# A fused metaformer block: the experts' bias as one 512-column product whose weights come back from DRAM, two small VectorE steps given to ScalarE, and the top-2 mask made in one step

## The reference

```python
t = _to_tokens(x)                                  # pixels x 128 channels
n = _ln_t(t)                                       # layer norm over channels
router_probs = softmax(n @ router_w + router_b)    # 8 experts
top_p, top_i = top_k(router_probs, 2)
top_p = top_p / sum(top_p)
expert_out = einsum('bnd,edc->bnec', n, expert_w) + expert_b
t = t + einsum('bnk,bnkc->bnc', top_p, take_along_axis(expert_out, top_i))
```

## Time and profile before

| | |
|---|---|
| time, median of 3 runs | 4167.12 us (4166.49 to 4171.71) |
| the profiled execution's own time | 4168.03 us |
| its span in the profile | 4166.2 us |
| mean granted TensorE clock | 0.957 |
| PE busy | 3877.1 us, 93% of the span |
| DVE busy | 2583.8 us, 62% |
| ACT busy | 1772.6 us, 43% |
| POOL busy | 1585.4 us, 38% |
| HBM traffic | 168 GB/s over the span |

### The profile page before, as it was taken

How to read it: one execution, slowest core, us unless ns; L and a number is a source line. 1 busy time by engine, 2 the same in 40 slices (tenths; PEclk the granted TensorE clock), 3 DMA queues, 4 the chain that set the end, 5 groups by cost and what they waited for, 6 DMA issues and landing times. The chain is left out here.

```text
span 4166.2 us, 90514 instructions
## 1 busy us (share of the span) xinstructions
PE 3877.1 (93%) x32471; PEld 2569.3 (62%) x32471; DVE 2583.8 (62%) x8765; ACT 1772.6 (43%) x4557; POOL 1585.4 (38%) x2857
## 2 busy tenths in 40 slices
PE   4999999999999999999978999999999999986458
PEld 4666666666666666666644555666666666654245
DVE  3444434444444444444428888999999999986634
ACT  3555545555555555555511111333333333356124
POOL 3544445454454544544412222332323232344210
PEclk8999999999999999999989999999999999999755
DMA  5544454444554544545416666777777777754869
GB/s 126 93 89 92 88 88 91 90 90 90 92 92 89 91 90 92 92 87 94 76 56 244 244 246 257 258 261 264 257 268 254 268 257 267 252 174 124 335 263 395
DMA packets 602226, 705.73 MB, mean 169 GB/s; under 512 B 61088, under 2 KB 484768, under 8 KB 585392
## 3 DMA queue, kind: packets, MB, share of 16 engines
q1 hardware_dynamic: 496304, 625.97, 52.6%
q10 hardware_dynamic: 104448, 71.85, 5.7%
q0 software_dynamic: 1024, 2.10, 0.1%
HBM read 519.10 MB, written 179.54 MB: 168 GB/s over the span
## 5 line engine op out<-in xcount | busy, mean ns | idle before, releaser
L366 PE MATMUL a_ob<-a_sr,wcv 128*128 128x512 f32 (+3 forms) x2820 | 1084.4, 519 | 0.8 <-DVE a_xo L496 0.8
L443 ACT COPY a_sr<-a_sb 128x576 f32<-128x576 f32 (+7 forms) x1296 | 620.9, 562 | 914.8 <-PE a_sb L351 906.6
L351 PEld LDWEIGHTS a_sb<-a_tt,a_win 32*128 32x128 f32 x19008 | 655.6, 185 | 260.0 <-issue 244.6
L351 PE MATMUL a_sb<-a_tt,a_win 32*128 32x144 f32 x19008 | 748.2, 300 | 14.5 <-ACT a_sr L443 13.1
L521 POOL TENSOR_TENSOR a_sx<-a_hh 128x576 f32<-128x576 f32 x260 | 378.5, 1456 | 927.3 <-DVE a_hh L473 919.2
L366 PEld LDWEIGHTS a_ob<-a_sr,wcv 128*128 128x128 f32 x2820 | 493.2, 192 | 279.6 <-issue 231.2
L473 DVE TENSOR_SCALAR a_hh<-a_hh 128x576 f32<-128x576 f32 (+1 forms) x128 | 59.5, 465 | 944.0 <-ACT a_hh L422 944.0
L1075 DVE TENSOR_TENSOR b_P<-b_P,b_x 128x1024 f32<-128x1024 f32 x512 | 620.0, 1212 | 0.1
L985 PE MATMUL b_z<-b_P,b_ew 128*128 128x512 f32 x1024 | 475.0, 607 | 0.0
L1206 POOL TENSOR_TENSOR b_ss<-b_st 128x12 f32<-128x12 f32 (+2 forms) x167 | 35.2, 211 | 1124.5 <-DVE b_pp L1150 993.5
L988 PE MATMUL b_z<-b_P,b_ew 128*128 128x512 f32 x1024 | 460.3, 592 | 0.0
(11 more groups left out here) (181 smaller groups left out, 5406.3 us busy)
## 6 DMA issues: line engine op xcount, KB each, us to landing
b_P<-pd SPq DMA_DIRECT2D x128, 2048.0 KB, 7.4
a_win<-xtp SPq DMA_DIRECT2D x2144, 36.0 KB
a_xin<-in_x SPq DMA_DIRECT2D x128, 256.0 KB, 5.9
xtp<-a_tn ACTq DMA_DIRECT2D x128, 256.0 KB, 2.3
x1d<-a_xo SPq DMA_DIRECT2D x128, 256.0 KB, 5.7
b_x<-x1d SPq DMA_DIRECT2D x128, 256.0 KB, 7.7
x2d<-b_xa SPq DMA_DIRECT2D x128, 256.0 KB, 2.8
d_wb<-in_w SPq DMA_DIRECT2D x16, 2048.0 KB, 18.8
```

Source lines behind the costliest of these rows:

```text
L351: t = e.matmul(d[:, 0:3 * m_, :, NU_ * i:NU_ * i + NU_], win[32 * q:32 * q + 32, half_of(Q, j) % NWH, NWIN // 3 * h + i, :], m, start=(j = ...
L366: t = e.matmul(ob[:, r:r + m, :], k["wcv"][:, 3 * (2 - kr) + kx, :], rows[:, :, t_, :], start=(t_ == 0 and r == 0), stop=(t_ == 8))
L443: a = e.copy(bass.AP(d.tensor, d.offset, [list(d.ap[0]), [1152, ni], [1536, nk], [32, 4], [1, m]]), bass.AP(v.tensor, v.offset, [list(v.ap ...
```

## The change

The bias of the experts becomes one matmul of 512 columns instead of four of 128. Its moving operand must have the experts on partitions and all 512 pixels along a row, which the transpose does not give (it gives (r, expert) on partitions). So `p_out` writes all 64 rows of `pT` to DRAM (32 KB, 16 before), and a new DMA `spread_b`, with lag 3, reads the 32 plain rows back as 8 partitions by 4 x 128 into a new tile `pb`. `pb` has two buffers and is cleared once, since the matmul takes all 128 partitions, as `ebm` now does. `pp` is 128 columns wide (64 of them stay zero), so its transpose takes a full tile of weights.

The copy of the logits from `RD` to `lr` goes from DVE to ACT, and so does the negated maximum `nm`. The mask and its product become one `scalar_tensor_tensor`: (`l2` is -3e38) times `ex`. A helper tensor `zero` moves to part A's memory.

```diff
-NX1, NPB, NPT = 9, 3, 4
+NX1, NPB, NPT, NPC = 9, 3, 4, 2
...
+        ("stats1", 0), ..., ("spread", 2), ("spread_b", 3), ("norm3", LAG + 1),
...
@@ tensor
-                e.transpose(X[0:64, 0:128], pp[:, u].rearrange("p a r x -> p (a r x)"), ident[:, :]
-                            ).then_inc(p_turned, 1)
+                e.transpose(X[:, 0:128], pp[:, u, :], ident[:, :]).then_inc(p_turned, 1)
...
-                for r in range(4):
-                    e.matmul(ZE[u][:, r, :], ebm[:, r, :], pT[0:32, G % NPT, :], start=(r == 0),
-                             stop=False)
+                w.wait_ge(pb_in[G % NPC], 16 * (G // NPC + 1))
+                e.matmul(ZE[u][:, :, :], ebm[:, :], pb[:, G % NPC, :], start=True, stop=False)
@@ scalar
+            if stage == "stats1":
+                w.wait_ge(stats1, G + 1)
+                w.wait_ge(r_step, R_STEPS * (G - 2) + 2)
+                e.copy(lr[:, u].rearrange("p (a b) x -> p a b x", a=2), RD[:, :, :, 128:136]).then_inc(lr_ready, 1)
...
-                e.copy(pT[:, G % NPT, :], X[0:64, 0:128]).then_inc(x_free, 1)
+                e.copy(pT[:, G % NPT, :], X[:, 0:128]).then_inc(x_free, 1)
...
-                w.wait_ge(neg_ready, 2 * G + 2)
+                w.wait_ge(top_ready, G + 1)
+                e.activation(nm[:, G % 3, :], cv[:, b, 8 * h:8 * h + 1], ACT.Copy, scale=-1.0).then_inc(nm_ready, 1)
+                w.wait_ge(nm_ready, G + 1)
                 w.wait_ge(best_ready, G + 1)
@@ vector
+        e.memset(pp[:, :, :], 0.0)
+        e.memset(pb[:, :, :], 0.0).then_inc(cleared, 1)
...
-                w.wait_ge(p_ready, G - 1)
-                e.tensor_copy(lr[:, u].rearrange("p (a b) x -> p a b x", a=2), RD[:, :, :, 128:136]
-                              ).then_inc(lr_ready, 1)
...
-                    e.tensor_tensor(mk[:, u], l2[:, u], lg[:, u], ALU.is_lt).then_inc(r_step, 1)
-                    w.wait_ge(r_step, n + 6)
                     w.wait_ge(exp_ready, G + 1)
-                    e.tensor_tensor(pm[:, u], ex[:, u], mk[:, u], ALU.mult).then_inc(w_step, 1)
+                    e.scalar_tensor_tensor(out=pm[:, u], in0=l2[:, u], scalar=-3.0e38, in1=ex[:, u],
+                                           op0=ALU.is_equal, op1=ALU.mult).then_inc(w_step, 1)
...
-                w.wait_ge(summed, G - 2)
-                e.tensor_scalar(nm[:, G % 3, :], v[:, 0:1], -1.0, None, ALU.mult).then_inc(neg_ready, 1)
@@ sync
-                e.dma_start(pd[G % NPT * 32:G % NPT * 32 + 32, :], pT[32:64, G % NPT, :]
+                w.wait_ge(pb_in[(G - NPT) % NPC], 16 * ((G - NPT) // NPC + 1))
+                e.dma_start(pd[G % NPT * 64:G % NPT * 64 + 64, :], pT[0:64, G % NPT, :]
...
+            elif stage == "spread_b":
+                w.wait_ge(p_out[G % NPT], 16 * (G // NPT + 1))
+                w.wait_ge(cleared, 1)
+                w.wait_ge(mixed, G + 1 - NPC)
+                e.dma_start(pb[0:8, G % NPC].rearrange("e (r x) -> e r x", r=4),
+                            pd[G % NPT * 64:G % NPT * 64 + 32, :].rearrange("(r e) x -> e r x", e=8)
+                            ).then_inc(pb_in[G % NPC], 16)
```

More of the change, by code:

```diff
@@ L831 @@
 NU = GI + XU
-NX1, NPB, NPT = 9, 3, 4
+NX1, NPB, NPT, NPC = 9, 3, 4, 2
 STEP = (("load", -3), ("load2", LAG - 2), ("read", 0), ("turn2", 6), ("fourier", LAG), ("turn3", LAG + 2),
         ("store2", 6), ("turn_p", 2), ("experts", 4), ("p_out", 2), ("scales", 1), ("best", LAG + 3), ("mixed", 5),
-        ("stats1", 0), ("stats2", 6), ("x3", LAG), ("store3", LAG), ("spread", 2), ("norm3", LAG + 1),
+        ("stats1", 0), ("stats2", 6), ("x3", LAG), ("store3", LAG), ("spread", 2), ("spread_b", 3), ("norm3", LAG + 1),
         ("gate", LAG + 2), ("experts2", 4), ("place", 5), ("sums", LAG + 3), ("weights", 1), ("turn_scale", 7),
@@ L883, in phase_bc @@
     S = lambda name, shape, dt=F32: ctx.enter_context(nc.sbuf_tensor(name, shape, dt))
-    ew = S("b_ew", [128, 8, 128]); iw = S("b_iw", [128, 136]); ebm = S("b_ebm", [32, 4, 128])
+    ew = S("b_ew", [128, 8, 128]); iw = S("b_iw", [128, 136]); ebm = S("b_ebm", [128, 128])
     rb = S("b_rb", [128, 8]); al = S("b_al", [128, 128]); gw = S("b_gw", [128, 2, 128]); gb = S("b_gb", [128, 1])
@@ L891, in phase_bc @@
     ex = S("b_ex", [128, 2, 4, 8]); mk = S("b_mk", [128, 2, 4, 8]); pm = S("b_pm", [128, 2, 4, 8])
-    sm = S("b_sm", [128, 2, 4]); rr = S("b_rr", [128, 2, 2, 4]); pp = S("b_pp", [128, 2, 2, 4, 8])
-    pT = S("b_pT", [64, NPT, 128])
+    sm = S("b_sm", [128, 2, 4]); rr = S("b_rr", [128, 2, 2, 4]); pp = S("b_pp", [128, 2, 128])
+    pT = S("b_pT", [128, NPT, 128]); pb = S("b_pb", [128, NPC, 512])
     xn = S("b_xn", [128, 2, 4, 128]); xa = S("b_xa", [128, 3, 4, 128]); rsr = S("b_rsr", [128, NG, 4])
@@ L910, in phase_bc @@
         sem(n) for n in ("read", "p_turned", "mixed", "turned2", "scale_turned", "filtered", "turned3", "gated"))
[L912 to L918, removed]
+    lr_ready, nm_ready, exp_ready, x_free, xa_ready, placed, tn3_ready, tnT3_ready, summed = (
+        sem(n) for n in ("lr_ready", "nm_ready", "exp_ready", "x_free", "xa_ready", "placed", "tn3_ready", "tnT3_ready", "summed"))
+    cleared, stats1, stats2, stats3, r_step, lm_ready, w_step, p_ready, z_ready, x2_ready, x3_ready, \
+        top_ready, best_ready = (sem(n) for n in (
+            "cleared", "stats1", "stats2", "stats3", "r_step", "lm_ready", "w_step", "p_ready", "z_ready",
+            "x2_ready", "x3_ready", "top_ready", "best_ready"))
     s_step, scaled = sem("s_step"), sem("scaled")
@@ L924, in phase_bc @@
     P_in = [sem(f"P_in{i}") for i in range(NPB)]
+    pb_in = [sem(f"pb_in{i}") for i in range(NPC)]
     x2_out = [sem(f"x2_out{i}") for i in range(3)]
@@ L1011, in tensor @@
                 e.matmul(X[:, 0:256], gw[:, 1, :], tnT3[:, u, 256:512], start=False, stop=True).then_inc(gated, 1)
+    R_STEPS = 5
     def scalar(e):
@@ L1018, in scalar @@
             u = G % 2
-            if stage == "weights" and G < NG:
+            if stage == "stats1":
+                w.wait_ge(stats1, G + 1)
+                w.wait_ge(r_step, R_STEPS * (G - 2) + 2)
+                e.copy(lr[:, u].rearrange("p (a b) x -> p a b x", a=2), RD[:, :, :, 128:136]).then_inc(lr_ready, 1)
+            elif stage == "weights" and G < NG:
                 w.wait_ge(lm_ready, G + 1)
@@ L1064, in scalar @@
                              accum_out=cs[:, b, h:h + 1]).then_inc(summed, 1)
-    R_STEPS = 6
     def vector(e):
@@ L1106, in vector @@
                     w.wait_ge(scaled, G + 1)
+                    w.wait_ge(lr_ready, G + 1)
                     e.tensor_tensor(lg[:, u], lr[:, u], rs[:, u, 4:8, None].to_broadcast([128, 4, 8]), ALU.mult
@@ L1149, in vector @@
                     w.wait_ge(p_turned, G - 1)
-                    e.tensor_tensor(pp[:, u], pm[:, u, None, :, :].to_broadcast([128, 2, 4, 8]),
+                    e.tensor_tensor(pp[:, u, 0:64].rearrange("p (a r x) -> p a r x", a=2, r=4),
+                                    pm[:, u, None, :, :].to_broadcast([128, 2, 4, 8]),
                                     rr[:, u, :, :, None].to_broadcast([128, 2, 4, 8]), ALU.mult).then_inc(p_ready, 1)
@@ L1182, in vector @@
                 w.wait_ge(x_free, users["gate", G] + 1)
-                e.max(v, lo[:, G % 3, :]).then_inc(neg_ready, 1)
-                w.wait_ge(neg_ready, 2 * G + 1)
-                w.wait_ge(summed, G - 2)
-                e.tensor_scalar(nm[:, G % 3, :], v[:, 0:1], -1.0, None, ALU.mult).then_inc(neg_ready, 1)
+                e.max(v, lo[:, G % 3, :]).then_inc(top_ready, 1)
+                w.wait_ge(top_ready, G + 1)
                 e.max_index(ci[:, b, 8 * h:8 * h + 8], v, lo[:, G % 3, :]).then_inc(best_ready, 1)
@@ L1231, in sync @@
             e.dma_start(t[:, :], ins[n][:, :]).then_inc(const_in, 16)
-        e.dma_start(ebm[:, :, :], ins["ebm"][:, :, :]).then_inc(const_in, 16)
+        e.dma_start(ebm[:, :], ins["ebm"][:, :]).then_inc(const_in, 16)
         for stage, G in order:
@@ L1247, in sync @@
                 e.dma_start(P[:, G % NPB].rearrange("p r e x -> p (r e x)"),
-                            pd[G % NPT * 32:G % NPT * 32 + 32, :].rearrange("a x -> (a x)").partition_broadcast(128)
+                            pd[G % NPT * 64 + 32:G % NPT * 64 + 64, :].rearrange("a x -> (a x)"
+                                                                                 ).partition_broadcast(128)
                             ).then_inc(P_in[G % NPB], 16)
+            elif stage == "spread_b":
[5 more added lines that the diff above has]
+                            ).then_inc(pb_in[G % NPC], 16)
             elif stage == "store2":
@@ L1649, in program @@
         k = {
-            "zero": S("zero", [128, 640]), "mhalf": S("mhalf", [128, 12]), "ones": S("ones", [128, 128]),
+            "mhalf": S("mhalf", [128, 12]), "ones": S("ones", [128, 128]),
             "ident": S("ident", [128, 128]), "fm": S("fm", [128, 2 * NG]),
@@ L1658, in program @@
         x3d = D("x3d", [B * H * W, 128])
```

(10 more changed lines are left out.)

## The result

| | before | changed |
|---|---|---|
| median | 4169.41 us (4 runs, 4166.49 to 4172.17) | 4130.12 us (4 runs, 4128.27 to 4135.2) |
| ratio | | 0.991, 95% interval 0.9896 to 0.9925 |
| profiled span | 4166.2 us | 4130.0 us |

The account below looks back on a forecast made before the run. VectorE was taken to bound the middle stage at 12.17 us a step, TensorE close behind at 12.04. Gains of 27.6 us there and 7.9 in the first stage, less 0.5 for clearing, gave 35.0 and 4132 us, range 4118 to 4157.

Parts of the forecast that it names:

- Who sets the pace: Middle stage of BC, 89 steps with both layers: VectorE sets the 12.17 us step; TensorE could do 12.04.
- VectorE's 11.79: Middle stage: VectorE's step after its three edits, 12.17 less 0.38 by distances of starts; by durations 11.63.
- The first stage: Layer 0 alone in BC: only the mask shortens VectorE's circle with GpSimd, 0.22 times 36 steps, 7.9 us.
- TensorE's step: Middle stage: the single bias product saves 0.18 us, so TensorE's step goes from 12.04 to 11.86.
- my best case for TensorE: Middle stage: TensorE's step if the two allowances, 0.11 and 0.03, cost nothing; 11.72 us.
- The DMA at nothing: Bias block's new read behind the spread of `P`: costed at nothing, with little to spare.
- The bound on x: Bias block lands x us after the spread of `P`, x between 0 and 0.57; 0.2 taken.
- the circle: Bias product, `ex`, `pp`, spread, block and back, over two steps: 22.92 + x us, 11.46 + x/2 each.
- The sum: Whole kernel: middle stage 27.6 us, first stage 7.9, last stage nothing, clearing 0.5; saving 35.0 us.
- The bias block comes late: Rival, middle stage: block pays its own landing, x = 2.2, step 12.56, 4194 us; slower from x = 1.6; chance 0.10.
- All of it: Rival: both lower ends, VectorE 11.63 and TensorE 11.72, 47 us less in all, 4120 us; chance 0.12.
- ScalarE, GpSimd, the last stage, the clearing: Side costs: ScalarE's added work and last stage (layer 1 alone) nothing, GpSimd 0.63 us to spare, clearing `pb` and `pp` 0.5.

Follow-up runs that it names:

- experiment 4: Kernel before with only VectorE's three edits (logits' copy and negated maximum on ScalarE, one-step mask), bias still four products; 4147.92 us, ratio 0.995.
- experiment 5: Changed kernel with VectorE's three edits undone, so the single bias product and its DMA alone; 4166.24 us, ratio 0.9995 to the kernel before.
- experiment 1: Changed kernel with the bias block's read issued ahead of the weights' write and the 2 MB spread; 4118.07 us, ratio 0.9884 to the kernel before.
- experiment 6: Kernel before with only the one-step mask; 4148.28 us in one run.
- experiment 7: Kernel before with only the logits' copy and the negated maximum moved to ScalarE; 4159.81 us in one run.
- experiment 2: Changed kernel with the bias block's read issued behind both 256 KB loads of the next step; 4195.95 us, ratio 1.0066 to the kernel before.
- experiment 8: Changed kernel with the bias block read early and the router's bias addition on VectorE left out; 4096.69 us, ratio 0.9833 to the kernel before.

## Why the prediction was right, point by point

**Who sets the pace** was right: VectorE before, TensorE at 12.04 close behind (experiment 4: 12.037), and so neither half alone gives the middle stage its whole gain: the bias product none of it (experiment 5), VectorE's edits 0.13 of 0.38 us a step (experiment 4).

**VectorE's 11.79**, by the distances of starts, was right to 0.01 us (experiment 1). By durations it would have been 11.63. The fixed term of the Trainium skill (VectorE: DVE Perf Modes, "The TRN2 errata") fits durations here (0.15 us for 128x1), but not what three instructions, taken out, gave back: 0.38 us where their durations sum to 0.51 (the 0.54 of the prediction took the mask at its distance, 0.22, and not at its duration, 0.19).

**The first stage** was right: 10.67 a step forecast and measured, all of it the mask (experiments 6 and 7: 10.66 and 10.88).

**TensorE's step** is the term that was mis-sized: 0.18 us saved where it was 0.42, so 11.62 and not 11.86. I added 0.11 for a start behind a wait and 0.03 for a wider transpose. A step that nothing holds has neither: the eight records of the experts take 3.43 instead of 3.54, so the 0.11 of the old kernel went with the four narrow products and was no wait (experiment 4 has it without one). And the transpose takes 0.11 instead of 0.21 before its successor, 0.10 that I had not seen at all. So even my best case for TensorE, 11.72, was too slow, and it is VectorE, not TensorE, that sets the pace afterwards. The middle stage would have gained 87 times 0.38, 33 us.

**The DMA at nothing** was wrong by 9.7 us (experiment 1), and this ate most of what TensorE gave beyond my term: 33.1 less 9.7 is 23.4, and 23.1 was measured (27.6 forecast, for 89 steps). The bound on x held: of 87 blocks none landed more than 0.28 us after its spread. What I left out is that the other term of the circle, the 7.6 us of the spread, is a median. With measured times the circle is 11.42 + x/2: 7.29 us from the bias product to `ex` instead of 7.50, and 0.13 more that I had forgotten, from the landing of the block to the start of the product. That is 11.5 with x = 0.2, but a spread of 9.1 us makes it 12.3.

**The sum** agreed with the result within 4 us of BC, and that is partly luck, because these two errors have opposite signs. That 4130.12 lies only 2 us from 4132 is luck once more: BC gave 3.2 us less than forecast, and what the medians show beyond it lies outside BC or is scatter between executions.

**The rivals.** "The bias block comes late" was the right mechanism at the wrong size: it happened in 15 steps, with x near 0 and not 2.2. Its threshold is real; experiment 2 stands at it (x = 1.57, where 1.6 was worked out) and is slower than before. The fixed cost of about 2.0 us that the Trainium skill gives (DMA: Bandwidth & Descriptors, "Anatomy of one DMA", a fit for DMAs that GpSimd issues, which these are not) was not paid afresh behind the spread: the median of x was 0.03. "All of it" came nearest for TensorE (11.72, measured 11.62) but had the wrong VectorE (11.63, measured 11.79).

**ScalarE, GpSimd, the last stage, the clearing**: nothing, nothing, -0.3 us and +0.3 us, against nothing, nothing, nothing and 0.5. The +0.3, from the first product to the first `pp`, need not be the clearing: experiment 4, which clears nothing more, has 9.39 us there. The clearing itself kept VectorE busy for 1.2 us (at the rate of L1161 it would be 2.15, not below 2.1), which ended 1.3 us behind the start of the first product.

## What to carry to other kernels

When two engines are both near full, take each engine's own step apart from its waits: a change that eases only one of them gives the distance to the other (here 0.13 of 0.38 us) and a change to the other alone gives nothing. Price a small VectorE instruction by how much later its neighbour starts, not by its duration. For a new DMA in a circle, work out the circle with its slow landings too; where a small block is needed soon and does not depend on the big transfer, issue it ahead of it (here one entry in the table, 12 us in the medians and 9.75 in the traces).

## What the runs showed of the hardware

**Spreads land later with instruction packets under way.** The profile lists two more queues beside SyncE's; of the changed kernel from 2700 to 3600 us (packets, MB, share of the 16 engines):

```profile
q1 hardware_dynamic: 150931, 242.22, 76.1%
q8 instruction: 30, 0.49, 0.2%
q14 instruction: 57, 0.47, 0.2%
```

I sorted the 2 MB spreads between 2650 and 3600 us by whether a packet of q8 or q14 was under way between issue and landing:

```
                  with such a packet          without              over 8.0 us: with / without
before            29 spreads, median 8.46     49, median 7.44      19 / 2
changed           46 spreads, median 8.39     34, median 7.44      31 / 1
block read early  45 spreads, median 8.32     35, median 7.41      31 / 1
```

Packets of 8 or 16 KB that fill 0.4% of the engines' time go with a spread that lands 0.9 to 1.0 us later. It is a correlation; the traces of experiments 4, 5 and 8 show it too (8.2 to 8.4 us with, 7.3 to 7.6 without). I did not vary the fetches.

**Landings out of order.** Where the spread was slow, the block issued behind it was at times there first: in the changed kernel 13 of 87 blocks landed 1.2 to 1.6 us before their spread. In all 13 the spread took 8.5 us or more. The semaphore of a spread had 16 updates, that of a block 9, of which one came 0.5 us after the issue and eight when the 8 rows landed. The Trainium skill (DMA: Bandwidth & Descriptors, "Queues, rings and completion order") says that completion is not first in, first out on one issuing engine, and that a copy may run on fewer than all of the engine's rings. The trace agrees.

**Four 128-column matmuls with 32 rows of weights cost more than one of 512 columns.** Behind them the 512-column experts took 3.54 us for eight records; behind one 512-column product of full height 3.43, and the transpose ahead 0.11 instead of 0.20. The four took 1.08 us where one takes 0.86 for as many columns. Whether the number of the products, the 32 rows or the width of the transpose ahead is the reason, no run here separates.
